# Attention and MoE block on one core: single norm tiles between exponentials, and two TensorE side tasks one pair of score passes later

## The reference

```python
x = x + _L0_attn_ref(_layernorm(x, axis=-1), Wq, bq, Wk, bk, Wv, bv, Wo, bo)
x = x + _L0_ffn_ref(_layernorm(x, axis=-1), Wr, br, W1, b1, W2, b2, gamma, beta)
# attention
Q, K, V = (proj(Wq, bq), proj(Wk, bk), proj(Wv, bv))
scores = jnp.einsum('bhqd,bhkd->bhqk', Q, K) * scale
attn = jax.nn.softmax(scores, axis=-1)
out = jnp.einsum('bhqk,bhkd->bhqd', attn, V)
# experts
logits = jnp.einsum('bsd,ed->bse', tgt, Wr) + br
top_v, top_i = jax.lax.top_k(logits, 2)
...
return _layer_norm(tgt + tgt2, gamma, beta)
```

## Time and profile before

| | |
|---|---|
| time, median of 3 runs | 650.49 us (648.87 to 650.55) |
| the profiled execution, its own time | 650.26 us |
| its span from the first to the last instruction | 648.4 us |
| busy in the span | PE 91%, DVE 75%, ACT 67%, POOL 36% |

### The profile page before, as it was taken

One profiled execution on the slowest core, in us unless ns is written; L12 is line 12 of the kernel. 1 busy time (PEld: TensorE's weight loads), 2 busy tenths in 40 slices (PEclk: granted clock), 3 DMA queues, 4 the chain that ended last, 5 costly groups with the idle time before them and its releaser, 6 DMA issues.

```text
span 648.4 us, 12762 instructions
## 1 busy us (share of the span) xinstructions
PE 591.1 (91%) x3656; PEld 320.6 (49%) x3656; DVE 486.0 (75%) x1287; ACT 436.7 (67%) x886; POOL 232.9 (36%) x397
## 2 busy tenths in 40 slices
PE   2889999999999999999999999999899999998872
PEld 1634333433343433343334343333399989988730
DVE  3577898999899999899899898896155444444358
ACT  2634788788788788888888877778664444443323
POOL 8110010022331422512512331231477775454445
PEclk9965999999999999999999999999999999999986
DMA  6751812212303302411331231113105222222172
GB/s 202 250 159 46 189 39 74 76 48 83 104 27 96 112 27 75 118 40 44 100 89 30 86 97 51 31 34 98 54 31 151 83 81 71 62 70 65 32 275 114
DMA packets 46622, 56.98 MB, mean 88 GB/s; under 512 B 8366, under 2 KB 25818, under 8 KB 46564
## 3 DMA queue, kind: packets, MB, share of 16 engines
q1 hardware_dynamic: 40580, 45.06, 24.3%
q0 software_dynamic: 4544, 8.53, 3.9%
q10 hardware_dynamic: 1440, 2.69, 1.2%
HBM read 29.28 MB, written 27.16 MB: 87 GB/s over the span
## 4 chain that ended last, share of the span: by engine, by line
PE 60%; DVE 20%; ACT 8%; issue 5%; POOL 3%; DMA 2%; DVEq 0%; SPq 0%; ACTq 0%; POOLq 0%
PE pv_psum L1063 12%; DVE mneg L770 10%; PE st_psum L993 10%; PE s_psum L977 10%; PE y_psum L1554 6%; ACT pt L651 4%; PE y_psum L1230 3%; PE side_psum L1025 2%; PE side_psum L999 2%; PE h_psum L1545 2%; PE side_psum L1019 2%; ACT xn L669 2%; PE h_psum L1547 2%; PE h_psum L1546 2%; DVE split L777 2%
## 5 line engine op out<-in xcount | busy, mean ns | idle before, releaser
L770 DVE TENSOR_REDUCE mneg<-s_psum 128x1 f32<-128x512 f32 x512 | 323.0, 684 | 31.6 <-PE s_psum L977 30.1
L651 ACT ACTIVATE pt<-st_psum 128x512 f32<-128x512 f32 x512 | 279.2, 598 | 68.3 <-PE st_psum L993 63.6
L977 PE MATMUL s_psum<-ks,qs 64*128 64x512 f32 x512 | 204.0, 472 | 3.0 <-DVE mneg L770 1.9
L993 PE MATMUL st_psum<-qs,ks 64*128 64x512 f32 x512 | 194.2, 458 | 8.1 <-ACT pt L651 7.7
L977 PEld LDWEIGHTS s_psum<-ks,qs 64*128 64x128 f32 x512 | 83.2, 190 | 108.8 <-DVE mneg L770 87.0
L1063 PE MATMUL pv_psum<-pt,vst 128*16 128x512 f32 x1024 | 134.5, 598 | 0.0
L993 PEld LDWEIGHTS st_psum<-qs,ks 64*128 64x128 f32 x512 | 79.8, 187 | 52.4 <-ACT pt L651 41.4
L1420 ACT ACTIVATE hid<-h_psum,b1c 128x384 f32<-128x384 f32 x68 | 36.9, 582 | 53.8 <-PE h_psum L1547 53.8
L1386 POOL DMA_INDIRECT results<-res,goal_now x51 | 49.9, 979 | 42.5 <-DVE res L1468 28.5
L510 POOL DMA_INDIRECT sent<-xrow,placeu x56 | 54.5, 974 | 16.2 <-issue 16.2
L1554 PE MATMUL y_psum<-w2t,hid 128*128 128x128 f32 x408 | 48.7, 275 | 1.2 <-DVE ysum L1462 1.2
(11 more groups left out here) (219 smaller groups left out, 803.2 us busy)
## 6 DMA issues: line engine op xcount, KB each, us to landing
parts<-split SPq DMA_DIRECT2D x48, 256.0 KB, 3.0
ks<-parts SPq DMA_DIRECT2D x128, 48.0 KB
qs<-parts SPq DMA_DIRECT2D x128, 48.0 KB
lot<-sent SPq DMA_DIRECT2D x18, 198.0 KB
sent<-tail SPq DMA_DIRECT2D x16, 198.0 KB, 5.0
xres<-in_L_attn_x_dram SPq DMA_DIRECT2D x8, 256.0 KB, 3.2
pt<-in_L_ffn_W_dram SPq DMA_DIRECT2D x1, 2048.0 KB, 14.1
got<-results SPq DMA_DIRECT2D x8, 256.0 KB, 6.3
```

What stands on the lines that cost most here:

```text
L651: nc.scalar.activation(pt[:, n % PT_SLOTS, (g + 2) % 4, :], st_psum[:, k % ST_BANKS, :], ACT.Exp, scale=SCALE).then_inc(exp_done, 1)
L770: nc.vector.tensor_reduce(mneg[:, (n // 4) % 2, at:at + 1], s_psum[:, k % S_BANKS, :], AX_X, ALU.max, negate=True).then_inc(max_done, 1)
L977: mm(s_psum[:, k % S_BANKS, :], qs[rows, c, P * (n % 4):P * (n % 4) + P], ks[rows, c, g, :], start=True, stop=True).then_inc(s_made, 1)
L993: mm(st_psum[:, k % ST_BANKS, :], ks[rows, c, g, P * (n % 4):P * (n % 4) + P], qs[rows, c, :], start=True, stop=True).then_inc(st_made, 1)
```

## The change

ScalarE: the first norm's tile 0 stays at the end of its beat, and tiles 1, 2 and 3 are issued in the next beat behind its first, second and third exponential. The second norm's tile 0 stays at the end of beat 13; tile 1 is issued behind the first exponential of beat 14, tile 2 behind the third, tile 3 stays at the end of that beat. The number and kind of instructions are the same. Signals are given by the last tile, as before.

TensorE: V (its first half) and the SHIFT of each batch's first quad (beat 4) are issued behind the third pair of score passes, where they stood behind the second. The other side tasks stay.

```diff
+def behind_split(kind, of):
+    return kind == "V" or kind == "SHIFT" and of % QUADS == 0
...
+        def first_normalise(b, j):
+            return nc.scalar.activation(xn_of(b)[:, j:j + 1, :], xres[:, tiles(b, j, 1), :], ACT.Identity,
+                                        bias=shift[:, j:j + 1], scale=rstd[:, j:j + 1])
...
                     nc.scalar.activation(pt[:, n % PT_SLOTS, (g + 2) % 4, :], st_psum[:, k % ST_BANKS, :], ACT.Exp,
                                          scale=SCALE).then_inc(exp_done, 1)
+                if g < 3 and (b := once(T, -15)) is not None:
+                    ins = first_normalise(b, g + 1)
+                    if g == 2:
+                        ins.then_inc(xn_done, 1)
+                if g in (0, 2) and (b := once(T, 30)) is not None:
+                    normalise(b, 1 + g // 2)
...
             if (b := once(T, -16)) is not None:
                 act.wait_ge(shift_done, b + 1)
-                for j in range(TILES):
-                    ins = nc.scalar.activation(xn_of(b)[:, j:j + 1, :], xres[:, tiles(b, j, 1), :], ACT.Identity,
-                                               bias=shift[:, j:j + 1], scale=rstd[:, j:j + 1])
-                ins.then_inc(xn_done, 1)
+                first_normalise(b, 0)
...
                 act.wait_ge(shift2_done, b + 1)
-                for j in range(2):
-                    normalise(b, j)
+                normalise(b, 0)
             if (b := once(T, 30)) is not None:
-                normalise(b, 2)
                 normalise(b, 3).then_inc(xn2_done, 1)
...
             scores_t(T, 1)
             for kind, of in early_tasks(T):
-                side(kind, of)
+                if not behind_split(kind, of):
+                    side(kind, of)
             scores_t(T, 2)
             scores(T, 2)
+            for kind, of in early_tasks(T):
+                if behind_split(kind, of):
+                    side(kind, of)
             scores_t(T, 3)
             scores(T, 3)
```

## The result

The changed kernel is slower: a median of 652.12 us (21 runs) against 650.57 us for the kernel before (21 runs), and a ratio of 1.0036 with a 95% interval of 1.0019 to 1.0053. The forecast was 646.9 us and faster; the time also lies outside the range that went with it. The medians are of all runs and the ratio of the fast ones alone, without a few that took 8 to 11 us more; the profiled execution of the changed kernel, 663.04 us, is one of these few.

The account below looks back on a forecast made before the run. TensorE was taken to hold 60% of the chain that ends last, VectorE 20%, ScalarE 8%. Terms 1.25 + 0.60 + 1.44 + 0.25 - 0.2 = 3.3 us off 650.26 gave 646.9 us, range 645.6 to 649.0.

Parts of the forecast that it names:

- "one gain only" rival: Beat 82: fourth exponential and XT come late behind the spread tiles, first norm's 1.85 us lost; 648.8 us, chance 0.18.
- First norm: Beats with exponentials: fewer tiles ahead of the first exponential; 1.25 us over five beats plus 0.60 for beat 17.
- the twin: Beats 113 and 114, last batch, no next batch to normalise: first to last pass 4.90 us, against 5.15 in beats 81 and 82.
- V: Beat 87 and five like it: TensorE's wait for Q's low part goes; 0.24 us each, 1.44 in all.
- beat 7: V's wait of 0.46 us in the first batch, worth 0.25 us (0.16 to 0.46).
- SHIFT: Beat 84: TensorE's 0.31 us wait goes, but VectorE's first maximum still sets the fourth pass; 0 us.
- The rival of 1.9 us: Beat 84: SHIFT's wait is worth something if VectorE's maximum were earlier too; 645.0 us, chance 0.06.
- Second norm: Beats 94 and 95: last tile up to 0.385 us later, X2T cover roughly 0.2; loss 0.03 us in 7 batches, 0.2.
- The 8.7 us of the rival: Second norm's last tile slips 1.34 us and X2T waits, 8.7 us lost over seven batches; 655.4 us, chance 0.07.
- Table loads: ScalarE: each switch between exponential and affine copy costs a table load, 82 us; 729 us, chance 0.01.
- Passing on: Chain of beats into the experts' part: nothing after beat 128 is reordered, so the 3.3 us pass whole.

Follow-up runs that it names:

- x1: Changed kernel with GpSimd's output-bias addition held until K of the same batch is copied out: 647.88 us against 648.54 before, ratio 0.9982.
- x4: Changed kernel with `gap` as four subtractions of one tensor and a per-partition scalar, addition not moved: 652.57 us against 648.54 before, ratio 1.0025.
- x5: Kernel before with the first norm's single tiles and the late bias addition: 647.36 us, one run; beats 16 to 127 355.23 us against 357.18.
- x6: Kernel before with V alone moved behind the third pair: 646.07 us, one run; beats 16 to 127 356.32 us against 357.18.
- x2: Kernel before with only GpSimd's bias addition held until K is copied out: 650.22 us against 648.54, ratio 1.0018.
- x8: Kernel before with only the SHIFT of each batch's first quad moved: 647.67 us, one run; beats 16 to 127 357.11 us against 357.18.
- x9: Changed kernel with the bias addition held behind K and the second norm's tiles put back: 645.18 us against 648.21 before, ratio 0.9969.
- x3: Kernel before with only GpSimd's bias addition held until it falls on `gap`: 654.94 us against 648.54, ratio 1.0074.
- x7: Kernel before with the second norm's tiles alone set singly: 651.07 us, one run; beats 16 to 127 357.70 us against 357.18.

## Why the prediction was wrong

**The step that failed** stands at the end of the working on the first norm: GpSimd's addition "moves with it; nothing reads its result before beat 11. I cost both at nothing". The move was seen and its readers were looked up, but not what the addition would then run *beside*. Its place in the trace before, 296.26 to 297.54, is among maxima, which read PSUM; behind the one that ends at 297.98 VectorE has the small instructions of the division and the routing, and 1.62 us later the addition meets them. The addition takes 1.28 us, the collision cost 4.83 us over five batches (x1 against after), and the forecast with that term is 646.9 + 4.8 = 651.7, against the 652.12 measured. That it comes so near is partly luck: over beats 16 to 127 the forecast's terms (-3.1) and the collision make +1.7 us, where +2.93 was measured, and most of the difference lies in V and the second norm. The "one gain only" rival named the right beat and the wrong mechanism: XT starts at 298.19, right behind VectorE's `onorm` (298.14), while the last norm tile had ended at 297.80, and 0.78 us into its beat, as in x1 (296.85 - 296.07), where nothing is lost.

The Trainium skill has a rule for just this. "SBUF — State Buffer", section "Who interferes with whom", says that a VectorE instruction with two SBUF inputs contends with a GpSimd instruction that reads SBUF, that one with at most one SBUF input outside some fast modes doesn't, and that `tensor_reduce` on this chip never does; the section "SBUF: two separate sides" calls the shared pair of ports an exclusive lock, held for the whole instruction. The runs agree in each point that they touch: 1.14 and 1.05 us for 0.15, ending 0.03 us behind the addition; 203 ns each in x4; a maximum of 0.69 us partly beside the addition as away from it. Laid beside the moved addition before the run, it would have priced the step at up to 1.28 us a batch, an estimate from the addition's duration.

**First norm: right in mechanism and size**, once the collision is away. 1.85 us were forecast, x5 gives 1.95; beats 81 and 82 end as the twin does. Beats 17 and 18, which have no routing and so no collision, take 6.49 us before and 5.88 after, 0.61 less where 0.60 was forecast.

**V: right in mechanism, the term mis-sized.** 0.24 us a beat were taken, 0.11 to 0.13 came (x6, after), half of it and below the lower end of 0.16. The working let the third pair follow the second and gain "something like" the 0.10 us that a lone pair loses. It doesn't quite follow. In the fence of beat 87 its two passes stand 315.88 - 315.61 = 0.27 us behind the second pair's start, so they do come close, but V then starts 0.43 us behind it, and V's second half 0.43 us behind the fourth pair (316.96 to 317.39): two pairs pay the price of a lone one, where the kernel before paid 0.32 for the second of two. The prediction saw in the 0.42 against 0.32 us of a lone pair the price of a change of tiling mode. The third pair follows two pairs of its own shape and pays 0.43 all the same, so these runs don't bear that reading out. ScalarE's row shows what the third pair waited for:

```profile
314.65 0.68 ACT L624 ACTIVATE split<-side_psum,bcols 128x512 fp32r<-128x512 f32 x1
315.22 2.86 ACT L660 ACTIVATE pt<-st_psum 128x512 f32<-128x512 f32 x5
```

The high part of Q stands ahead of the last exponential of beat 86, which begins at 315.22 and takes 0.6 us; the pass that needs its bank begins at 315.88. That this exponential is the reason is read from the times; no run took it away. Over beats 16 to 127 x6 shows 0.86 us of the 1.44 forecast for six beats.

For beat 7, 0.25 us were taken. Where TensorE's clock is full for most of that beat, it takes 3.79 us without the move (x2, x8) and 3.66 or 3.67 with it (x6, x9, after). Where it is half throughout, as in the earlier trace rows, it takes 5.30 (before, x3, x5, x7) and 5.27 (x1, x4). So the term was worth 0.12 or 0.03 us.

**SHIFT: right.** Nothing was forecast, and the 0.07 us of x8 can't be told from nothing (x2 differs by 0.06): the fourth pass waits for the first maximum, which did not move. The rival of 1.9 us is out.

**Second norm: right in sign, the term mis-sized.** 0.2 us of loss were taken in all, x7 shows 0.52. The last tile ends at 341.09, 1.00 us into beat 95, where it was 0.69 before; the cover did not hold it all, and X2T waits 0.42 us. Beat 95 grows by 0.06 us, so the cover was about 0.26, near the 0.2 that was taken. What the term missed is beat 111. The cover is VectorE's: in beat 95 it has the statistics of the next first norm ahead of the maxima, here in the kernel before,

```profile
339.79 0.87 DVE L735 BATCH_NORM_STATS2 stats<-xres 128x6 f32<-128x128 f32 x4
```

and in beat 111, with no batch left to normalise, there is no such instruction. So beat 111 doesn't repeat beat 95, as was said ahead of the prediction: in the kernel before it takes 4.03 us against 4.30, and it passes the whole slip on, 0.32 us. That the statistics are the cover is read from the times of these two beats; no run took them away. The 8.7 us of the rival needed a slip of 1.34 us and had 0.31. In company the loss is 0.81 us (x1 against x9): 0.33 in beats 31 to 95, 0.31 in beat 111, and the rest in differences of under 0.03 us a beat.

**Table loads: out.** The run after has one load, as before:

```profile
L609 ACT ACT_TABLE_LOAD  x1: 1283/1283/1283, 0.8 to 0.8; - x1
```

**Passing on.** The forecast let the beats' gain through to the end whole. As far as the intervals go it does: that of each of x1, x3 and x9 holds the beats' difference. Only x3's is narrow enough to shut out half of it (0.47 to 1.02%, for 0.69).

**The range.** The forecast's better end, 4.4 us, is given as V's upper ends without the second norm's loss. Those make 1.25 + 0.60 + 1.92 + 0.46 = 4.2; the 4.4 takes the upper ends of the first norm as well. Nothing hangs on it, since the time came out on the other side.

## What to carry to other kernels

When a signal moves, list everything that waits for it, on every engine, and ask of each not only who needs its result but what it will run beside: for a GpSimd operation on SBUF the question is whether VectorE has an instruction with two SBUF inputs in its new window, however small. A short instruction that suddenly takes a microsecond, and ends with one on another engine, is the trace's sign of it; shifting the off-path operation by one wait was worth 4.8 us here. Where the start of a program varies by more than the change is worth, compare a stretch of repeating beats and let the total confirm it.

## What the runs showed of the hardware

VectorE's subtraction of two SBUF tensors, 128 x 4, is held until GpSimd's 128 x 512 addition is over: 1.04 to 1.14 us for 0.15, in the ten executions of after and x3 that meet it. Maxima from PSUM, a product of one PSUM and one SBUF tensor (`onorm`, 0.29 us with 0.26 us of it beside the addition, as before) and subtractions with a per-partition scalar are not.

How long TensorE runs at half clock during the start differs between profiles: 27.3 us before, 20.5 in the changed kernel, 17.1 in x2. Two stretches of the start, before and, in the second fence, after:

```profile
40.00:60.00 20.00, 18.35 (x41) 7.70 (x40) 13.99 (x24) 5.59 (x11) 0.00 (x0) 0.50 0.40 128
60.00:85.00 25.00, 23.58 (x143) 8.92 (x141) 22.06 (x41) 18.80 (x38) 0.00 (x0) 0.91 0.57 130
```

```profile
40.00:60.00 20.00, 18.06 (x44) 7.63 (x43) 14.21 (x25) 6.11 (x12) 0.00 (x0) 0.57 0.42 129
60.00:85.00 25.00, 22.84 (x147) 8.45 (x145) 23.05 (x47) 19.30 (x40) 0.63 (x3) 1.00 0.59 130
```

The granted clock is 0.50 (all of it at the 1.2 GHz level) and 0.91 of the full 2.4 GHz in one, 0.57 and 1.00 in the other. And x2, whose start is that of the kernel before but for the late addition, begins beat 16 at 81.40 us where the kernel before begins it at 84.99. A difference of 3.6 us in the start is larger than the 2.93 us that the whole change is worth, which is why the beats from 16 on carry the comparison.
